# Linear-attention stage of a four-layer kernel: the token sum taken before v's projection, with a new order of the queues

## What is computed

```python
QKV = jnp.einsum('bsd,ed->bse', X, W_in) + b_in      # X: the normalised x
Q, K, V = jnp.split(QKV, 3, axis=-1)
Q = rope(Q, rot_dim); K = rope(K, rot_dim)           # rot_dim = 128 of 256
A = jnp.sum(feature_map(K) * V, axis=-2)             # feature_map: K / |K| per token; sum over tokens
Y = A[:, None, :] * Q
Y = jnp.einsum('bsd,ed->bse', Y, W_out) + b_out      # and Y + X, and x + that
```

## Time and profile before

| | us |
|---|---|
| median of 3 runs | 589.16 (586.92 to 590.02) |
| profiled execution | 586.79 |
| its span, first to last instruction | 584.9 |
| granted TensorE clock, share of full | 0.998 |

### The profile page before, as it was taken

How to read it: one execution, slowest core, us unless ns; L and a number is a source line. 1 busy time by engine, 2 the same in 40 slices (tenths; PEclk the granted TensorE clock), 3 DMA queues, 4 the chain that set the end, 5 groups by cost and what they waited for, 6 DMA issues and landing times.

```text
span 584.9 us, 12978 instructions
## 1 busy us (share of the span) xinstructions
PE 568.9 (97%) x4180; PEld 535.1 (91%) x4180; DVE 477.4 (82%) x1467; ACT 371.8 (64%) x1043; POOL 221.4 (38%) x325
## 2 busy tenths in 40 slices
PE   7999999999999999999999999999999999899995
PEld 7899999999999999999999999999998988788884
DVE  4789779778967897797789778877887989778885
ACT  5786557656765756576556657657887756554552
POOL 3666223223323332332233233323447778513220
PEclk9999999999999999999999999999999999999999
DMA  8802400000000000000000000000000000001011
GB/s 313 299 2 101 126 2 2 1 1 0 0 0 0 0 0 0 0 0 0 0 0 0 0 0 0 0 0 1 1 1 1 1 2 1 2 0 37 18 33 60
DMA packets 9136, 14.71 MB, mean 25 GB/s; under 512 B 1552, under 2 KB 6672, under 8 KB 9104
## 3 DMA queue, kind: packets, MB, share of 16 engines
q1 hardware_dynamic: 9104, 14.30, 7.0%
HBM read 12.20 MB, written 2.10 MB: 24 GB/s over the span
## 4 chain that ended last, share of the span: by engine, by line
PE 84%; DVE 7%; POOL 3%; ACT 2%; issue 2%; DMA 0%; POOLq 0%; DVEq 0%
PE bank L629 68%; PE bank L715 5%; PE bank L729 5%; PE bank L732 2%; PE bank L639 2%; PE bank L824 1%; ACT prob L1099 1%; DVE pT L1710 1%; DVE prob L1501 1%; DVE raw L1694 1%; DVE prob L1703 1%; DVE prob L1479 1%; POOL qkv L464 1%; DMA x<-in_x 0%; PE bank L893 0%
## 5 line engine op out<-in xcount | busy, mean ns | idle before, releaser
L508 POOL TENSOR_SCALAR prob<-prob,rowinv 128x128 f32<-128x128 f32 (+1 forms) x128 | 96.9, 769 | 275.5 <-DVE rowinv L1495 275.5
L629 PE MATMUL bank<-xT,big 128*128 128x256 f32 x984 | 129.3, 283 | 0.1
L629 PEld LDWEIGHTS bank<-xT,big 128*128 128x128 f32 x984 | 123.4, 192 | 1.0 <-issue 0.2
L1099 ACT ACTIVATE prob<-prob,negmax 128x128 f32<-128x128 f32 (+1 forms) x256 | 112.8, 445 | 7.8 <-DVE negmax L1479 7.8
L629 PE MATMUL bank<-wp,oT 128*128 128x256 f32 x768 | 102.3, 283 | 0.0
L629 PEld LDWEIGHTS bank<-wp,oT 128*128 128x128 f32 x768 | 96.9, 190 | 0.7
L1061 ACT ACTIVATE qT<-bank 128x512 fp32r<-128x512 f32 x68 | 40.6, 598 | 76.8 <-PE bank L629 76.8
L629 PE MATMUL bank<-pT,v 128*128 128x512 f32 (+1 forms) x384 | 79.9, 343 | 0.2
L629 PEld LDWEIGHTS bank<-pT,v 128*128 128x128 f32 x384 | 63.1, 189 | 9.9 <-issue 0.7
L1433 DVE TENSOR_TENSOR pT<-bank,pT 128x512 fp32r<-128x512 f32 (+1 forms) x128 | 65.2, 551 | 2.4 <-ACT pT L1061 2.3
L1061 ACT ACTIVATE pT<-bank 128x512 fp32r<-128x512 f32 (+1 forms) x128 | 55.2, 484 | 12.0 <-PE bank L729 9.5
(11 more groups left out here) (165 smaller groups left out, 973.0 us busy)
## 6 DMA issues: line engine op xcount, KB each, us to landing
x<-in_x SPq DMA_DIRECT2D x8, 256.0 KB, 7.9
raw<-in_wq SPq DMA_DIRECT2D x4, 512.0 KB, 8.2
raw<-in_wp SPq DMA_DIRECT2D x4, 512.0 KB, 8.2
out<-x SPq DMA_DIRECT2D x7, 256.0 KB, 2.1
raw<-in_w_gu SPq DMA_DIRECT2D x2, 640.0 KB, 5.2
raw<-in_w_in SPq DMA_DIRECT2D x1, 768.0 KB, 4.5
raw<-in_w_down SPq DMA_DIRECT2D x1, 640.0 KB, 7.1
raw<-in_wk SPq DMA_DIRECT2D x1, 512.0 KB, 3.8
```

The costliest lines, as they stand in the source:

```text
L508: m = pool.tensor_scalar(prob[:, j % 2, 0, a:b], prob[:, j % 2, 0, a:b], rowinv[:, j % 2, r:r + 1], None, ALU.mult)
L629: m = pe.matmul(out, lhs(a), rhs(b), start=first and i == 0, stop=last and i == len(passes) - 1, skip_group_check=True)
L1099: m = act.activation(prob[:, j % 2, i, a:b], prob[:, j % 2, i, a:b], ACT.Exp, scale=-1.0, bias=negmax[:, 2 * i + r:2 * i + r + 1], accum_o ...
```

## The change

For every batch, sum over tokens of k/|k| times v equals the row-wise product of v's weights with G = sum over tokens of k (x/|k|)^T. So V is no longer projected:

- PE projects K alone, 256 columns wide, both token tiles into one bank (`linear_k`). The bias is added by DVE when it copies the bank (`k_copy`); ACT squares from that copy (`k_squares`).
- POOL writes 1/|k| as a 257th column beside x/|k|, which ACT makes (`weigh`, from `xns`, of which there are two now). PE makes G with four plain fp32 matmuls of 257 columns (`linear_sum` on PE, two banks). DVE multiplies each bank by v's weights and bias (`wv_bias`) and sums along the row, straight into A (`linear_sum` on DVE).
- v's weights are transposed once in batch 7 (`order_wv`, `linear_wv`, `pick_v_bias`); they aren't split any more, and the bias split goes.
- x is normalised two batches ahead into `xns[n % 2]`.
- The orders change: PE in period n: K(n), out(n-2), transpose(n+1), sum(n-1), q(n); the last period ends with out(6) and sum(7). DVE: q products(n-1), k copy(n), k cosine(n), add(n-2), x lo(n+1), sum(n-1), y lo(n-1), apply(n+2), extras. ACT: squares(n), x hi(n+1), weigh(n), y(n-1), q(n). POOL: q rotate(n-1), k sine(n), k inverse(n), k rotate(n), bias(n).

```diff
-        kv = flat_prob[:, 1024:1536].rearrange("p (t d) -> p t d", t=ST)
+        XW = ST * (D + 1)
+        xw = [flat_prob[:, q * XW:(q + 1) * XW].rearrange("p (t d) -> p t d", t=ST) for q in range(2)]
         gate = flat_prob[:, 0:512]
...
-            def k_rotate(n):
+            def k_sine(n):
 
                 q = n % 2
                 k = k_sb[q][:, :, 0:P].rearrange("p t (e i) -> p t e i", e=2)
                 sin = rope[:, 1, :, 0, :].rearrange("p t (i e) -> p t e i", e=2)
-                pool.wait_ge(s_lke, ST * n + ST)
+                pool.wait_ge(s_lke, n + 1)
                 for e in range(2):
                     m = pool.tensor_tensor(k_sin[q][:, :, e, :], k[:, :, 1 - e, :], sin[:, :, e, :], ALU.mult)
                 m.then_inc(s_lks, 1)
+
+            def k_rotate(n):
+
+                q = n % 2
+                k = k_sb[q][:, :, 0:P].rearrange("p t (e i) -> p t e i", e=2)
                 pool.wait_ge(s_lks, n + 1)
                 pool.wait_ge(s_lkc, n + 1)
+                pool.wait_ge(s_lsq, n + 1)
                 pool.tensor_tensor(k, k_cos[q], k_sin[q], ALU.add).then_inc(s_lr, 1)
 
...
-                if n > 0:
-                    pool.wait_ge(s_lkv, n)
-                pool.tensor_tensor(k_inv[:, :], k_bound[:, :], exponent[:, 0:ST], ALU.pow).then_inc(s_lki, 1)
+                if n > 1:
+                    pool.wait_ge(s_lG, 2 * n - 2)
+                pool.tensor_tensor(xw[n % 2][:, :, D:D + 1], k_bound[:, :].rearrange("p (t o) -> p t o", o=1),
...
             def linear(n):
+                if n > 0:
+                    q_rotate(n - 1)
+                k_sine(n)
+                if n >= NB - 2:
+                    inv_std(n + 2)
+                k_inverse(n)
+                k_rotate(n)
                 if n == 1:
                     inv_std_twice(NB - 1)
-                if n >= NB - 2:
-                    inv_std(n + 2)
-                k_rotate(n)
-                k_inverse(n)
-                q_rotate(n)
-                if n == 0:
-                    linear_bias(0)
-                if n == 4:
+                if n == 5:
                     linear_scale(NB - 1)
-                if n < NB - 1:
-                    linear_bias(n + 1)
+                linear_bias(n)
...
             for n in range(NB):
                 linear(n)
+            q_rotate(NB - 1)
 
 
...
+            def linear_wv():
+
+                pe.wait_ge(s_vlo, 2 * NB)
+                pe.wait_ge(s_rawl[0], 16)
+                pe.wait_ge(s_wvo, 1)
+                for k in range(KT):
+                    pe.transpose(bM[:, k * P:(k + 1) * P], wv_pairs[:, k, :], ident[:])
+                    m = pe.transpose(bM[:, D + k * P:D + (k + 1) * P], raw_v[:, k, P:D], ident[:])
+                m.then_inc(s_wvp, 1)
...
+            bK, bA = (bS0, bS1), (bT0, bT1)
+
+            def linear_k(n, t):
+
+                if t == 0:
+                    pe.wait_ge(s_llo, n + 1)
+                    if n < 2:
+                        pe.wait_ge(s_inlo, 2)
+                        pe.wait_ge(s_mx, 2 * J * NB)
+                    else:
+                        pe.wait_ge(s_lke, n - 1)
                 for k in range(KT):
-                    mm3(pe, out[:, :], lambda a: xTs[n % 2][:, a, k, t * P:(t + 1) * P], lambda a: lin_w[:, a, k, D:3 * D],
-                        k == 0, False)
-                pe.matmul(out[:, :], mean_rows, kv_bias, start=False, stop=True, skip_group_check=True).then_inc(s_kvp, 1)
+                    m = mm3(pe, bK[n % 2][:, t * D:(t + 1) * D], lambda a: xTs[n % 2][:, a, k, t * P:(t + 1) * P],
+                            lambda a: lin_w[:, a, k, D:2 * D], t == 0 and k == 0, t == ST - 1 and k == KT - 1)
+                if t == ST - 1:
+                    m.then_inc(s_lkp, 1)
 
...
-                pe.wait_ge(s_lkv, n + 1)
+                pe.wait_ge(s_lxs, n + 1)
+                pe.wait_ge(s_lr, n + 1)
                 if n == 0:
-                    pe.wait_ge(s_olo, J * NB)
+                    pe.wait_ge(s_pTlo, 2 * J * NB)
                 else:
-                    pe.wait_ge(s_lAc, n)
-                if n == 2:
-                    pe.wait_ge(s_fz, NB)
-                if n == 3:
-                    pe.wait_ge(s_fa, NB)
-                if n == NB - 1:
-                    pe.wait_ge(s_flag, 1)
+                    pe.wait_ge(s_lA, 2 * n)
                 for e in range(2):
                     for t in range(ST):
-                        m = pe.matmul(bO[:, e:e + 1], kv[:, t, e * P:(e + 1) * P], ones[:, 0:1], start=t == 0, stop=t == ST - 1)
-                m.then_inc(s_lA, 1)
+                        m = pe.matmul(bA[e][:, 0:D + 1], k_sb[n % 2][:, t, e * P:(e + 1) * P], xw[n % 2][:, t, :],
+                                      start=t == 0, stop=t == ST - 1)
+                    m.then_inc(s_lG, 1)
...
                 if n > 1:
-                    linear_kv(n, 0)
+                    linear_k(n, 0)
+                    linear_k(n, 1)
+                    linear_out(n - 2)
+                else:
+                    linear_sum(n - 1)
                 linear_transpose(n + 1) if n + 1 < NB else gated_transpose(0)
-                linear_sum(n - 1)
-                linear_kv(n, 1)
                 if n == 2:
-                    pe.wait_ge(s_lAc, n)
                     ternary_transpose(NB - 1)
                 if n == 3:
-                    pe.wait_ge(s_lAc, n)
+                    pe.wait_ge(s_fz, NB)
                     ternary(NB - 1, bO)
                 if n == NB - 1:
                     pe.wait_ge(s_los, 4)
-                    pe.wait_ge(s_lAc, n)
+                    pe.wait_ge(s_fa, NB)
                     pe.matmul(bO[:, 8:12], ones[:, :], lo_sums[:, :], start=True, stop=True).then_inc(s_lop, 1)
+                if n > 1:
+                    linear_sum(n - 1)
                 linear_q(n)
                 if n == NB - 1:
                     gated_transpose(1)
-                linear_out(n - 1)
+                    linear_out(n - 1)
+                    linear_sum(n)
 
...
+            def k_squares(n):
+                act.wait_ge(s_lke, n + 1)
+                if n > 0:
                     act.wait_ge(s_lkb, n)
-                m = act.activation(k_square[:, t, :], out[:, 0:D], ACT.Square, accum_out=k_norm[:, t:t + 1])
-                if t == ST - 1:
-                    m.then_inc(s_lsq, 1)
+                for t in range(ST):
+                    m = act.activation(k_square[:, t, :], k_sb[n % 2][:, t, :], ACT.Square, accum_out=k_norm[:, t:t + 1])
+                m.then_inc(s_lsq, 1)
+
+            def weigh(n):
+
+                act.wait_ge(s_lki, n + 1)
+                for t in range(ST):
+                    m = act.activation(xw[n % 2][:, t, 0:D], xns[n % 2][:, t, :], ACT.Copy,
+                                       scale=xw[n % 2][:, t, D:D + 1])
+                m.then_inc(s_lxs, 1)
...
             def linear_y(n):
-                act.wait_ge(s_lA, n + 1)
-                if n > 0:
-                    act.wait_ge(s_lylo, n)
-                act.activation(A_sb[:, :], bO[:, 0:2], ACT.Copy).then_inc(s_lAc, 1)
-                act.wait_ge(s_lAc, n + 1)
                 act.wait_ge(s_lqr, n + 1)
                 if n > 0:
                     act.wait_ge(s_lo, n)
+                    act.wait_ge(s_lylo, n)
+                else:
+                    act.wait_ge(s_op, J * NB)
                 for e in range(2):
-                    act.activation(yT[:, 0, e, :], q_sb[n % 2][:, e, :], ACT.Copy, scale=A_sb[:, e:e + 1]).then_inc(s_lyhi, 1)
+                    act.wait_ge(s_lA, 2 * n + e + 1)
+                    act.activation(yT[:, 0, e, :], q_sb[n % 2][:, e, :], ACT.Copy, scale=A_sb[:, e:e + 1]).then_inc(s_ly, 1)
 
             def linear(n):
-                linear_k(n, 0)
+                if n > 1:
+                    k_squares(n)
                 linear_x_hi(n + 1, (n + 1) % 2) if n + 1 < NB else gated_x_hi(0)
+                weigh(n)
                 linear_y(n - 1)
-                linear_k(n, 1)
+                linear_q(n)
                 if n == 2:
                     ternary_hi(NB - 1)
-                linear_q(n)
                 if n == NB - 1:
                     gated_x_hi(1)
-                if n < NB - 2:
-                    linear_residual(n + 2)
+                if n < NB - 1:
+                    linear_residual(n + 1)
...
+            def k_copy(n):
+                dve.wait_ge(s_lkp, n + 1)
+                if n == 0:
+                    dve.wait_ge(s_bk, 1)
+                dve.tensor_tensor(k_sb[n % 2], bK[n % 2][:, :].rearrange("p (t d) -> p t d", t=ST),
+                                  b_k.rearrange("p (o d) -> p o d", o=1).to_broadcast([P, ST, D]), ALU.add).then_inc(s_lke, 1)
...
+            def linear_sum(n):
+
+                if n == 0:
+                    dve.wait_ge(s_wv, 1)
+                else:
+                    dve.wait_ge(s_lylo, n)
+                    dve.wait_ge(s_lA, 2 * n)
```

(113 more changed lines are left out.)

120 lines of the change are left out of this document (49 added, 71 removed).

## The result

| | before | after |
|---|---|---|
| median, us | 588.29 (586.92 to 590.02) | 596.75 (596.47 to 596.95) |
| profiled execution, us | 586.8 | 596.7 |
| its span, us | 584.9 | 594.9 |
| granted TensorE clock | 0.998 | 0.989 |

The ratio is **1.0151, 95% interval 1.0119 to 1.0182**: 1.5% slower. The forecast was 599.2, in a range of 591 to 605.

A forecast was written before the change was run, and what follows sets the result against it. PE and DVE were taken to share the bound. PE loses 6.5 us of matmul work, but the added wait decides: the layout gives +9.1, with collisions +11.6, taken as +10 on 589.2, so 599.2 us, range 591 to 605.

The forecast's parts named there:

- The sum's high end: On PE, the new sum's 8 records cost two streams of columns each, 1.76 us; 1.72 was taken.
- the forecast +4.0: DVE's own work in the linear stage grows by 0.5 us per batch, over eight batches.
- The added wait: In each period y(n-1) waits for the next batch's inverse norm: 3.7 us from k_copy's end to y low.
- The layout: Four engine queues placed by hand in the new order through the linear stage: out(7) 9.1 us later, collisions left out.
- "This decides.": The added wait for the next batch's inverse norm sets the linear stage's period, 7.55 us plus extras against PE's 6.5.
- Rival (c): POOL's bias add collides with y low in six periods, +6 on the +9: 604 us; chance 0.13.
- (a): PE decides the linear stage and the chain hides: about 10 us less, 579; chance 0.08.
- (b): Waits on y are hidden and DVE's own list decides: about 590 us, no change; chance 0.10.
- Rival (d): PE's clock falls to 1.2 GHz behind a 3.6 us hole before the second gated transpose: 603 us; chance 0.12.
- The base: The median of three runs of the kernel before, 589.2 us, on which the forecast stands.

The follow-up runs named there:

- experiment 5: The changed kernel run once more as it is, beside others on the same chip: 596.5 us, ratio 1.0157 against the kernel before.
- experiment 1: The changed kernel with ACT making y(n-1) ahead of weigh(n): 597.83 us, ratio 1.0188 against the kernel before.
- experiments 3 and 4: Kernel before plus one DVE instruction in periods 1 to 7: 590.79 us, ratio 1.0067; kernel before with old sums' matmuls issued twice: 590.89 us, ratio 1.0064.

## Why the prediction was right, and where it was not

**PE's work.** The sum's high end held: its 8 records take 1.63 us to the next start (478.08 to 479.71), 1.72 taken. The Trainium skill, "FP8 and Floating Point Precision", section "TensorE Precision Notes", has four passes for true fp32; 4 matmuls x 257 columns x 4 passes at 2.4 GHz, one column to a cycle, is an estimate of 1.71 us by that page, and the trace agrees with 1.63.

**DVE's work.** `k_copy` takes 0.72 us to the next start (0.60 taken, 0.75 was the high end), the reductions 0.69 (0.70 taken). The page of the profile has DVE at 482.2 us busy against 477.4 before, +4.8 for the forecast +4.0, with what the held instructions add.

**The added wait.** From the end of `k_copy` (480.29) to y low (483.97) is 3.68 us; 3.7 was predicted. The period of batch 4, from q products to q products, is 9.9 us and not 8.6: y low and apply, taken at 0.95 and 0.85 in that layout, took 1.84 and 1.27 to the next start, which is the whole difference.

**The layout.** Placed and found, in us:

| | T(3) | T(4) | T(5) | T(6) | T(7) | gated 0 | gated 1 | first tile | out(7) |
|---|---|---|---|---|---|---|---|---|---|
| placed | 456.7 | 467.2 | 477.6 | 486.9 | 495.5 | 505.7 | 514.2 | 517.8 | 522.4 |
| found | 456.98 | 468.55 | 477.64 | 488.21 | 496.92 | 508.14 | 515.74 | 520.86 | 524.73 |

The loss at out(7) is 11.4 us, where 9.1 (layout) to 11.6 (with collisions) stood. The hole before the second gated transpose is 2.51, not 3.6: DVE released it 1.5 us later than placed, but PE came to it 2.6 us later. Periods took 7.6 to 11.6 us, wider than the 8.6 to 10.4 named. Behind out(7) 1.4 us come back (70.2 us to the end of the span against 71.6). That is the last output DMA: from the start of the last DVE instruction to the end of the span are 2.6 us after and 4.1 before. It is chance and not the change: in the second profiled execution (experiment 5), without the third dip, out(7) starts at 523.07, a loss of 9.7, and nothing comes back (71.5 us).

**The step that failed** is the sentence "This decides." The wait was predicted to its size and place, and taking it away gave nothing (experiment 1). It and the collision with the bias add end in the same instant (with y first the pairs of periods 2 to 4 end within 0.05 us of where they ended, the later ones 0.2 to 0.4 earlier), so they aren't terms of a sum. Rival (c) had the right mechanism and the wrong arithmetic: it put the collisions on top of the wait, at +6 for six periods, while they run beside it, and hold the end of y low when the wait is gone; in the changed kernel the six pairs are 3.5 us longer than 0.88 each, and the one of period 5 isn't held at all, since `linear_scale` stands there in front of the bias add. The apply, which the prediction counts with y low among the instructions of two SBUF inputs, has one tensor input, and was stretched too: in period 4 beside L535, and in period 5 its first instruction took 1.37 us instead of 0.40 beside the bias add. The forecast was right in size partly by luck, because the two ends lie close: the layout, counting the wait alone, has y low of batch 4's period end at 485.3, and held by POOL it ended at 485.89. With the wait called the cause, the remedy would have been wrong too: the obvious one (experiment 1) is worth 0, the other 4.6.

**Rivals (a) and (b)** fell. PE had up to 3.9 us of holes in a period, and took 13 us of more work for 2 to 3. DVE had holes too. The reading of the earlier trace rows that two engines share the bound of the kernel before was borne out by experiments 3 and 4. **Rival (d)** came true as an event, behind shorter holes than it asked for, and hardly as a price: 1.65 us in one profiled execution, nothing in the other, where +4 was put. The Trainium skill, "TensorE: Matmul & The Clock Gate", section "HAM oscillation — how this bites in real kernels", has idle stretches put the clock back. The traces agree for the holes of 1.75 and 1.93 us; a hole of 1.97 us (out at 467.01) was followed by no dip, and that of 2.5 us by one in only one of two executions. A dip cost only what lay on the path.

**The base** was 0.9 too high (589.2 for 588.3). Between the profiled executions the difference is +9.9 (596.7 less 586.8), close to the +10 of the forecast; between the medians it is +8.5, since the profiled execution before lies 1.5 under its median and the one after on it.

## What to carry to other kernels

Where an instruction ends late both because it waits and because it is held, remove each alone and both together before calling one the cause: here 0, 4.6 and 6.3 us. That POOL is only 37% busy doesn't make its instructions free: look at which two-input DVE instructions run beside them, and whether another engine can absorb one (a bias into a PE accumulation took 0.24 us a batch and paid). And when two engines share a bound, work saved on one can be lost again on the other's chain: here an estimated 6.5 us less on PE, and 8.5 us more in all.

## What the runs showed of the hardware

- y low, a DVE instruction with two SBUF inputs, is held by a running POOL tensor_tensor over 256 to 512 elements and ends 0.28 us behind it, whether it started 0.5 us earlier or later (experiment 1). One over two elements didn't hold it. A pair over 256 elements took up to 2.67 us instead of 0.87.
- The granted clock fell to 1.2 GHz behind holes of 1.75, 1.93 and 2.51 us, in periods in which PE was busy for 67 to 73%. Behind a hole of 1.97 us in the same kernel it didn't fall, and of two executions with the same schedule only one had the third dip.
- The end of a span depends on how fast the last output DMA lands. In the second profiled execution of the changed kernel the last DVE instruction starts at 590.61, in the first at 592.30, yet the spans are 594.6 and 594.9. The output DMAs' times from issue to landing, the first execution and then the second:

```profile
DMA to landing us min/median/max: 1.7/2.1/2.2
```

```profile
DMA to landing us min/median/max: 1.7/2.1/3.2
```
